# All sixteen magnitude jobs of the last phase run inside its scan loop, their results parked in the normalised-input buffer

## What is computed

```python
xn = _layernorm(x, axis=-1)
# attention-like part
delta = softplus(einsum('btd,ed->bte', xn, Wd) + bd)
a_pos = softplus(a_log) + 0.0001
def step(state, inp):                       # over time
    x_t, delta_t = inp
    dt = delta_t[:, :, None]
    a_bar = jnp.exp(-dt * a_pos[None])
    state = a_bar * state + dt * b_param[None] * x_t[:, :, None]
    return (state, state.sum(-1))
attn = einsum('btd,ed->bte', y, Wo) + bo
# magnitude part
real = einsum('bti,io->bto', xn, cos(theta + theta_noise))
imag = einsum('bti,io->bto', xn, sin(phi + phi_noise))
ffn = sqrt(real * real + imag * imag)
out = x + attn + ffn
```

## Time and profile before

| | us |
|---|---|
| median of 3 runs | 1110.69 |
| lowest and highest run | 1108.01, 1128.71 |
| the profiled execution | 1109.44 |
| its span, slowest core (core 0) | 1107.5 |
| spans of the eight cores | 1095.8 to 1107.5 |

### The profile page before, as it was taken

How to read it: one execution, slowest core, us unless ns; L and a number is a source line. 1 busy time by engine, 2 the same in 40 slices (tenths; PEclk the granted TensorE clock), 3 DMA queues, 4 the chain that set the end, 5 groups by cost and what they waited for, 6 DMA issues and landing times.

```text
span 1107.5 us, 9304 instructions; the slowest of 8 cores (1095.8 to 1107.5 us)
## 1 busy us (share of the span) xinstructions
PE 578.0 (52%) x2248; PEld 242.3 (22%) x2248; DVE 818.6 (74%) x721; ACT 582.2 (53%) x924; POOL 154.2 (14%) x127
## 2 busy tenths in 40 slices
PE   1323334445467554555545447655655554455785
PEld 1211011111123330222212114433222211121343
DVE  4269888989842349999999992434799999999423
ACT  4775767666633235656665553323366555565330
POOL 2477000000012100000000001211000000000232
PEclk9975565656668765666665668988666556665799
DMA  8777100000011310000000002231000000000023
GB/s 231 214 224 206 43 29 29 28 20 1 0 48 59 122 37 0 1 1 0 1 0 1 0 0 66 85 114 57 29 1 0 1 0 0 1 0 1 29 72 114
DMA packets 36323, 51.65 MB, mean 47 GB/s; under 512 B 3120, under 2 KB 19760, under 8 KB 36272
## 3 DMA queue, kind: packets, MB, share of 16 engines
q1 hardware_dynamic: 33584, 42.68, 13.5%
q0 software_dynamic: 2688, 8.39, 2.2%
HBM read 42.67 MB, written 8.39 MB: 46 GB/s over the span
## 4 chain that ended last, share of the span: by engine, by line
DVE 41%; PE 21%; issue 17%; ACT 16%; DMA 2%; DVEq 1%; POOL 0%; ACTq 0%; SPq 0%; POOLq 0%
DVE grot L807 34%; ACT abar L758 9%; PE pd L930 6%; PE pt L649 3%; PE pd L296 3%; PE pt L659 3%; DVE sfm L944 2%; ACT bdg_bf L177 2%; DMA xsub<-xin 1%; PE pe L377 1%; DMA abar<-xin 1%; PE py L958 1%; DVE xsub L439 1%; PE py L377 1%; PE pt L377 1%
## 5 line engine op out<-in xcount | busy, mean ns | idle before, releaser
L807 DVE TENSOR_TENSOR_SCAN grot<-abar,gcar,vbuf 128x768 bf16<-128x768 f32 (+1 forms) x380 | 652.2, 1778 | 43.9 <-ACT abar L758 31.7
L758 ACT ACTIVATE abar<-delta,nega 128x768 f32<-128x768 f32 (+1 forms) x380 | 336.7, 896 | 242.8 <-DVE grot L807 241.2
L845 PE MATMUL pe<-grot,bdg_bf 128*128 128x384 bf16 x256 | 86.8, 444 | 119.2 <-DVE grot L807 119.2
L845 PE MATMUL py<-grot,bdg_bf 128*128 128x384 bf16 x256 | 84.8, 438 | 119.3 <-DVE grot L807 119.2
L296 PE MATMUL pd<-xnbf,wd_bf 128*128 128x384 bf16 (+1 forms) x368 | 97.4, 445 | 20.6 <-ACT xsub L315 14.7
L930 PE MATMUL pd<-ybf,wo_bf 128*128 128x384 bf16 (+1 forms) x320 | 74.8, 385 | 0.0
L832 PE MATMUL py<-grot,bdg_bf 128*128 128x512 bf16 x64 | 33.1, 527 | 79.6 <-DVE grot L807 79.6
L699 POOL TENSOR_TENSOR xsub<-r,i 128x384 f32<-128x384 f32 (+1 forms) x9 | 18.1, 2010 | 384.4 <-ACT i L691 384.4
L649 PE MATMUL pt<-xnbf,cos_bf 128*128 128x384 bf16 (+1 forms) x320 | 70.8, 370 | 0.0
L832 PE MATMUL pe<-grot,bdg_bf 128*128 128x512 bf16 x64 | 34.2, 546 | 68.2 <-DVE grot L807 68.2
L659 PE MATMUL pt<-xnbf,sin_bf 128*128 128x384 bf16 (+1 forms) x320 | 67.8, 359 | 0.0
(11 more groups left out here) (110 smaller groups left out, 566.8 us busy)
## 6 DMA issues: line engine op xcount, KB each, us to landing
xsub<-xin SPq DMA_DIRECT2D x14, 512.0 KB, 4.2
xres<-xin SPq DMA_DIRECT2D x32, 192.0 KB, 2.5
out<-osub POOLq DMA_DIRECT2D x32, 192.0 KB, 2.7
xres<-xin SPq DMA_DIRECT2D x8, 256.0 KB, 3.9
out<-osub POOLq DMA_DIRECT2D x8, 256.0 KB, 3.2
etmp<-tht SPq DMA_DIRECT2D x6, 256.0 KB, 4.8
r<-thn SPq DMA_DIRECT2D x6, 256.0 KB, 5.9
r<-pht SPq DMA_DIRECT2D x6, 256.0 KB, 3.9
```

The lines of the kernel that those rows point to most:

```text
L758: sx = run("scalar", lambda e, sl=sl_ab, par=par, dt=dt, n=n, tp=tp: e.activation(out=abar[:, sl * TP:sl * TP + tp], in_=delta[:, par * TP ...
L807: vs = run("vector", lambda e, g=gsl, sl=sl_ab, par=par, dt=dt, n=n, tp=tp: e.tensor_tensor_scan(out=grot[:, g * TP:g * TP + tp], data0=ab ...
L845: td = run("tensor", lambda e, c=c, g=gsl, dt=dt, n=n, bb=ypair[c]: e.matmul(bb[:, 0:384], bdg_bf[:, (dt * NST + n) * P:(dt * NST + n + 1) ...
```

## The change

For the last phase alone (`p == NPH - 1`):

- `NFC` becomes `nch` (16): the tail issues no job any more.
- The matmuls of job `2*dt` stand at the start of block `dt`. Three entries are added at the end of `aux`: the chain of job `2*dt`, the matmuls of job `2*dt + 1`, the chain of job `2*dt + 1`. In blocks 1 to 6 they come behind Exp 7, 8 and 9; in block 0, which has no copies to `ybf`, behind Exp 5, 6 and 7; in block 7, which has no softplus pieces, behind Exp 3, 4 and 5. The chain at the block's end is gone.
- Jobs 5 to 15 keep their result in 512-column pieces of `xn32` instead of ring slots in `delta`, `vbuf` and `abar` (`P2SLOT`, `rslot2`). POOL waits there for the writers of `xn32` and `xnbf` of the phase and for the product that last read the rows the piece lies in. Jobs 0 to 4 keep their ring slots.

Phases 0 and 1 are as before.

```diff
--- before.py
+++ after.py
@@ -518,8 +518,9 @@
                    + [vbuf[:, j * 512:(j + 1) * 512] for j in range(3)]
                    + [abar[:, j * 512:(j + 1) * 512] for j in range(3)])
         NRING = len(ring_ap)
-        ring_stt = [0] * NRING
-        ring_g = [0] * NRING
+        ring_ap = ring_ap + [xn32[:, 512 * s:512 * s + 512] for s in range(12)]
+        ring_stt = [0] * (NRING + 12)
+        ring_g = [0] * (NRING + 12)
         gadd_ev = [winit_last_g, winit_last_g]
 
         a_done_set = [set() for _ in range(NPH + 1)]
@@ -610,6 +611,13 @@
             ffn_ti = [0]
 
             def ring_avail_waits(j, eng):
+                if j >= NRING:
+                    s = j - NRING
+                    wait(eng, "V", a_x32_v[p])
+                    wait(eng, "S", a_xnbf_s[p])
+                    for r_ in range((512 * s) // TP, (512 * s + 511) // TP + 1):
+                        wait(eng, vv_done[r_][0], vv_done[r_][1])
+                    return
                 if j < 3:
                     par = 0 if j == 0 else 1
                     wait(eng, "T", ev_xT_free[par])
@@ -675,9 +683,17 @@
                     return i
                 return i - NRING + 3
 
+            P2SLOT = {5: 3, 6: 5, 7: 0, 8: 1, 9: 2, 10: 4,
+                      11: 6, 12: 7, 13: 8, 14: 9, 15: 10}
+
+            def rslot2(i):
+                if p == NPH - 1 and i in P2SLOT:
+                    return NRING + P2SLOT[i]
+                return rslot(i)
+
             def emit_ffn_chain(i):
                 dt, c0, wdth = cjobs[i]
-                j = rslot(i)
+                j = rslot2(i)
                 li = i % 2
                 tr, ti = ffn_mm[i]
                 wait("scalar", "T", tr)
@@ -708,10 +724,16 @@
                 mag_exp[i] = run("scalar", lambda e, w=wdth, a=ring_ap[j]: e.activation(
                     out=a[:, 0:w], in_=a[:, 0:w], func=AF.Exp, scale=0.5), "S")
 
-            ffn_at = ({6: [0], 7: [1]} if p == 0
-                      else {0: [0], 1: [1], 2: [2], 3: [3], 4: [4],
-                            5: [], 6: [5], 7: [6]})
-            NFC = 2 if p == 0 else 7
+            if p == 0:
+                ffn_at = {6: [0], 7: [1]}
+                NFC = 2
+            elif p == NPH - 1:
+                ffn_at = {dt_: [2 * dt_] for dt_ in range(NDT)}
+                NFC = nch
+            else:
+                ffn_at = {0: [0], 1: [1], 2: [2], 3: [3], 4: [4],
+                          5: [], 6: [5], 7: [6]}
+                NFC = 7
             yev_pend = []
             for dt in range(NDT):
                 par = dt % 2
@@ -731,6 +753,10 @@
                 if p == 0 and dt < 2:
                     for q_ in range(4):
                         aux.append(("diag", dt + 6, q_))
+                if p == NPH - 1:
+                    aux.append(("fch", 2 * dt, 0))
+                    aux.append(("fmm", 2 * dt + 1, 0))
+                    aux.append(("fch", 2 * dt + 1, 0))
                 if p == 0 and 2 <= dt < 6:
                     aux.append(("sinc", (dt - 2) * 4, 4))
                 if p == 0 and dt in (0, 1, 6, 7):
@@ -797,6 +823,10 @@
                             ev_d = emit_diag_s(adt, ac * 4, ac * 4 + 4)
                             if ac == 3:
                                 bdg_ev[adt] = ("S", ev_d)
+                        elif kind == "fmm":
+                            emit_ffn_mm(adt)
+                        elif kind == "fch":
+                            emit_ffn_chain(adt)
                     if hoisted:
                         vs = hoist_vs[n]
                     else:
@@ -855,8 +885,9 @@
                 for c in ([0] if p == 0 else [0, 1]):
                     yev_mm[(dt, c)] = td_c[c]
                     yev_pend.append((dt, c))
-                for jb in ffn_at.get(dt, []):
-                    emit_ffn_chain(jb)
+                if p != NPH - 1:
+                    for jb in ffn_at.get(dt, []):
+                        emit_ffn_chain(jb)
                 if p == 0:
                     for _ in range(3):
                         if wo_cast_jobs:
@@ -934,7 +965,7 @@
                         start=(k == 0), stop=(k == NDT - 1)),
                         "T" if k == NDT - 1 else None)
                 slot = it % 2
-                jr = rslot(it)
+                jr = rslot2(it)
                 wait("vector", "T", tw)
                 wait("vector", "S", mag_exp[it])
                 wait("vector", "LI", 16)
```

## The result

| | before | after |
|---|---|---|
| median, us (8 runs each) | 1108.74 | 1127.04 |
| lowest and highest run | 1107.19, 1128.71 | 1123.93, 1132.56 |
| the profiled execution | 1109.44 | 1126.31 |
| its slowest core | 0, span 1107.5 | 6, span 1124.8 |
| last phase, scan loop (scan 4 of block 0 to the end of the last scan) | 242.9 | 284.2 |

The ratio of after to before is 1.0164, with a 95% interval of 1.014 to 1.0187: slower, by less than 2%. The run of 1128.71 before and one run of experiment 4 (1116.69) are slow ones and stand in no comparison. The forecast of 1128 was right, and the two halves of the sum have the signs it gave them: +41.3 us in the loop and -24.1 in the tail, together +17.2, against +17.3 in the spans. The rest of the program moved by 0.1 us (scan 4 starts at 789.2 instead of 789.3). After the change the same two lengths stand in seven of the eight cores.

A forecast was written before the change was run, and what follows sets the result against it. VectorE's scans were taken to bound the last phase's loop, TensorE being busy for most of the tail. From 1109.4, +40.3 us in the loop and -21.6 in the tail gave 1128.1 us; range 1120 to 1139.

The forecast's parts named there:

- the two halves of the sum: Last phase: scan loop +40.3 us (35 to 47), tail behind it -21.6 us.
- Rival 2: Tail: TensorE stays at 1.2 GHz, so every step is slow; 1149 us with all slow, chance 0.08.
- Rival 3: Scan loop: bigger stalls, burst never seeing the clock rise and first chain losing cover; 1139 us, chance 0.16.
- Rival 4: Scan loop: ScalarE's three-buffer lead absorbs the second chain, only POOL's 0.70 per added job paid; 1094 us, chance 0.06.
- The stall before scan 10: Last-phase blocks: VectorE waits for Exp 10, queued behind the second chain; 4.95 us a block, used for all eight.
- the burst: Second job's 16 matmuls after scan 7: 4.64 us, the middle of 3.95 and 5.32.
- block 5's 0.70: Block 5 had no chain before, so the first chain's price there is not offset: +0.7 us.
- Blocks 0 and 7: Same 4.95 us stall used though places differ and cover is less; a miss of 1 to 2 us each allowed.
- The first chain behind Exp 7: Blocks 1 to 6: no wait before scan 8; price 0.70 us, offset by 0.70 saved at the block's end.
- The 0.36 us of cover: Before scan 8: product and copy between scans 7 and 8 hide the first chain with 0.36 us to spare.
- The tail: Behind the loop, without jobs: first sum at 1037.0, one 4.28 interval and 14 of 2.76; -21.6 us.
- The rule cited in the prediction: TensorE clock: full clock earned by continuous work, lost through idle gaps; taken strictly, tail gains 0.3 us, not 21.6.

The follow-up runs named there:

- experiment 4: Changed kernel with the matmuls of the last phase's eight odd jobs left out, chains kept (output not the reference's): profiled execution 1095.95 us.
- experiment 1: Changed kernel with the odd job's chain moved from behind Exp 9 to the block's end, its matmuls unmoved: 1093.32 us.
- experiment 7: Experiment 2 with the odd job's POOL add waiting for scan 15, its Ln and Exp behind the next block's Exp 9: 1084.87 us, 0.9779 of before.
- Experiment 2: Changed kernel with odd chains at the block's end and first chains behind Exp 7 in blocks 0 and 7 too: 1093.30 us, 0.9874 of before.
- experiment 5: Kernel before without the last phase's jobs 7 to 15, the tail re-adding magnitudes of jobs 0 to 6 (output not the reference's): 1084.79 us.
- 6: Experiment 2 without POOL's add in the last phase, ScalarE taking Ln of the first square plus 1 (output not the reference's): 1080.59 us.
- experiment 3: Changed kernel with the odd job's chain two Exps later (behind Exp 11 in blocks 1 to 6), its matmuls unmoved: 1102.76 us.

## Why the prediction was right, step by step

The chance stood at 0.72 for a time within 2%, the range held, and rivals 2, 3 and 4 did not happen. But four terms were off: two made the forecast too low, by 3.4 and 1.3 us, two too high, by 3.6 and 2.5. The signs, the place of the stall and the range are earned; that 1128 and 1127 lie so close is luck. Lengths of the blocks (block 0 from scan 4 on), us:

| block | 0 | 1 | 2 | 3 | 4 | 5 | 6 | 7 | sum |
|---|---|---|---|---|---|---|---|---|---|
| before | 24.21 | 31.54 | 31.54 | 32.01 | 31.54 | 30.90 | 31.54 | 29.60 | 242.9 |
| after | 27.06 | 36.84 | 37.29 | 37.42 | 37.48 | 37.57 | 37.50 | 33.02 | 284.2 |
| more | 2.85 | 5.30 | 5.75 | 5.41 | 5.94 | 6.67 | 5.96 | 3.42 | 41.3 |
| forecast | 4.95 | 4.95 | 4.95 | 4.95 | 4.95 | 5.65 | 4.95 | 4.95 | 40.3 |

- **The stall before scan 10: right in mechanism, too small.** Over blocks 1 to 6 it is 33.1 us instead of 6 x 4.95 = 29.7, 11% more. In block 1 the links from the end of scan 7 (831.20) are, in the prediction's order, 0.15 + 0.59 + 5.02 + 0.10 + 2.39 + 0.43 + 1.09 = 9.77 against the 9.41 that it summed; less 4.46 that is 5.31. The mis-sized term is the burst: 4.64 was taken as the middle between 3.95 and 5.32, and it was 5.02 in block 1, 5.27 in block 2 (868.99 to 874.26) and 5.33 in block 5. Timeline of TensorE in block 2, core 6, the cos matmuls at the block's start and the burst after scan 7; then, from experiment 1 (core 6, block 1), a burst at the same place:

```profile
857.35 1.46 PE L657 MATMUL pt<-xnbf,cos_bf 128*128 128x384 bf16 x8
...
868.99 2.76 PE L657 MATMUL pt<-xnbf,cos_bf 128*128 128x384 bf16 x8
871.55 2.71 PE L667 MATMUL pt<-xnbf,sin_bf 128*128 128x384 bf16 x8
```
```profile
825.61 2.48 PE L657 MATMUL pt<-xnbf,cos_bf 128*128 128x384 bf16 x8
827.92 1.46 PE L667 MATMUL pt<-xnbf,sin_bf 128*128 128x384 bf16 x8
```

  At the block's start the job's matmuls stand behind the 16 of the projection and run at 2.4 GHz (granted clock 1.00), 1.46 us for eight. After scan 7 they come behind single pairs, and the granted clock is 0.50 in the first half of the burst and 0.54 in the second: it rises only at its end. That isn't a property of the place. In experiment 1 a burst at the same place took 3.77 (825.61 to 829.38, mean clock 0.73), in experiment 7 such bursts took 3.8 to 5.3, and in the kernel before the projection, which also stands behind single pairs, took 3.95, 4.12, 4.19, 4.36, 4.59 and 5.23 in its six blocks (core 0). Where in a burst the clock rises differs from block to block. What the middle of two rows could not show is that in this kernel, with blocks of 37.3 to 37.6 us, the bursts of blocks 2 to 6 all took 5.27 to 5.33, on every core. Why the clock always rose so late there isn't shown.
- **Late TensorE at block starts: missing from the sum.** In blocks 2 to 6 scan 4 starts 0.2 to 0.4 us late, on `py` or `pe` (the row at 860.61). It needs the `grot` buffer of scan 0, so the pair of scan 0 must be done, and that pair stands behind 32 matmuls in TensorE's queue. They stood there before as well; what is new is how long the projection takes, since the clock rises later in it. Timelines of TensorE: before, core 0, block 3, and after, core 6, block 2 (block 2 before: 3.95):

```profile
876.07 5.23 PE L296 MATMUL pd<-xnbf,wd_bf 128*128 128x384 bf16 x16
```
```profile
852.55 4.96 PE L296 MATMUL pd<-xnbf,wd_bf 128*128 128x384 bf16 x16
```

  In the traces of all nine kernels, on all cores, a block with job matmuls at its start has the wait where the projection takes more than 4.8 us, and hasn't where it takes less; block 5 of experiment 5, with no job there, has none even at 5.32. Before it was block 3 alone, with 0.48; now it is blocks 2 to 6 (4.96 to 5.18). Net 1.3 us. With the longer stalls (33.1 instead of 29.7) and block 5's 0.70, which was right, blocks 1 to 6 cost 35.0 and not 30.4.
- **Blocks 0 and 7: over-priced by 3.6 us.** The prediction used 4.95 and allowed a miss of 1 to 2 each, without the sign. In block 0 the second chain stands behind Exp 7, under the product's cover, and its sin matmuls take 1.46 at the full clock: the wait before scan 8 is 1.41. In block 7 the second job's burst runs at the full clock as well, and its chain costs a wait of 0.61 and 0.69 on a scan; the first chain, behind Exp 3, costs a wait of 2.27 and 0.54 on a copy. Experiment 2 shows what moving the first chain under the product's cover saves: 0.7 in block 0 and 1.7 in block 7.
- **The first chain behind Exp 7: right.** No wait before scan 8 in blocks 1 to 6, POOL's add 2.28 us, price 0.70. The 0.36 us of cover held.
- **The tail: right in kind, 2.5 us better.** The first sum comes 4.88 after the last scan (4.8 by the prediction's sum). No interval was slow (1.5), and a step is 2.69, not 2.76 (15 x 0.07 = 1.0). The 0.07 is in the wait before the sum, 0.60 instead of 0.67. I take it to be one semaphore wait less on VectorE: the program issues a wait only where the event isn't known to be past already, and in after all magnitudes are. Two rows bear it out. In experiment 5 the only step of 2.75 among the 2.69 ones is the one that reads job 6, whose root is the last of the loop; and in experiment 7, as in 1, 2 and 6, it is the last, of job 15, the only one finished behind the loop:

```profile
1074.78 0.62 DVE L992 SCALAR_TENSOR_TENSOR sfm<-pd,csts,xn 128x384 f32<-128x384 f32 x1 [0.60 <-PE pd L978]
...
1077.54 0.62 DVE L992 SCALAR_TENSOR_TENSOR sfm<-pd,csts,xn 128x384 f32<-128x384 f32 x1 [0.67 <-PE pd L978]
```

  That the extra wait itself takes the 0.07 is argued, not tried.
- **Rival 2, the tail at 1.2 GHz.** The mechanism exists, but ends after three steps at most. Core 5 of experiment 2, VectorE's second and third sum, TensorE's transposes at either clock, and then the table of stretches of the same core:

```profile
1041.45 0.62 DVE L978 SCALAR_TENSOR_TENSOR sfm<-pd,csts,xsub 128x384 f32<-128x384 f32 x1 [1.86 <-PE pd L964]
...
1045.75 0.62 DVE L978 SCALAR_TENSOR_TENSOR sfm<-pd,csts,xsub 128x384 f32<-128x384 f32 x1 [1.86 <-PE pd L964]
```
```profile
1042.21 0.88 PE L992 MATMUL py<-csts,sfm 128*128 128x128 f32 x3 [0.87 <-DVE sfm L978]
...
1053.51 0.52 PE L992 MATMUL pe<-csts,sfm 128*128 128x128 f32 x3 [0.87 <-DVE sfm L978]
```
```profile
1042.00:1046.00 4.00, 3.44 (x11) 1.70 (x11) 0.87 (x3) 0.00 (x0) 0.76 (x1) 0.50 0.24 76
...
1050.00:1060.00 10.00, 6.57 (x41) 4.05 (x42) 4.49 (x8) 0.00 (x0) 2.28 (x3) 0.98 0.45 137
```

  At a clock of 0.50 sums are 4.30 us apart, and TensorE stands idle for 0.87 in each step; after three such steps it is at 0.98 and stays there with the same 0.87 idle in each step of 2.69. Three steps cost 3 x 1.61 = 4.8 us. The rule cited in the prediction (the Trainium skill, TensorE: Matmul & The Clock Gate, section Why this matters for your kernels) wants continuous work to reach the full clock; word for word that doesn't hold here, since the clock rose through a gap in every step. What the page says of losing the clock is about long idle gaps only, which the prediction left out; the gaps here are under 1 us, and the clock held through them, as the page has it. How many slow steps a tail has (0, 1, 2 or 3) differs from kernel to kernel and core to core; what decides it is left open.
- **Rival 3** (1139) had the burst right (5.3), but charged 0.7 a block for a lost cover that held, and made blocks 0 and 7 dearer where they were cheaper. **Rival 4** (1094) is near what experiment 1 gives (1093.32), though its mechanism did not happen: the lead of three buffers did not absorb the chain where it stood, and POOL's 0.70 per job is the price only once the order is mended.

## What to carry to other kernels

Work put into a gap of an engine that looks idle (ScalarE was busy 140 of 243 us) costs by where it stands in that engine's queue: everything behind it waits until its latest input is there. Count from the event that releases its producer, not from its own length, and put it where the next consumer has to wait anyway, or split it so that each piece stands behind its input. When a burst on TensorE is priced, read many such bursts and not two: 16 matmuls of 384 columns behind single pairs took 3.8 to 5.3 us here, by where the clock rose in them, and in the changed kernel nearly all lay at the upper end. So give such a term its whole range.

## What the runs showed of the hardware that I had not expected

**POOL's add and VectorE's instructions take turns.** VectorE's scans 8 and 9 and POOL's add in experiment 4, then VectorE's scan 11 and copy and POOL's add in experiment 3 (timelines, core 0 and core 1):

```profile
827.31 1.81 DVE L837 TENSOR_TENSOR_SCAN grot<-abar,gcar,vbuf 128x768 bf16<-128x768 f32 x1
829.04 2.49 DVE L837 TENSOR_TENSOR_SCAN grot<-abar,gcar,vbuf 128x768 bf16<-128x768 f32 x1
828.48 1.43 POOL L715 TENSOR_TENSOR etmp<-r,i 128x384 f32<-128x384 f32 x1 [3.84 <-ACT i L707]
```
```profile
832.65 1.80 DVE L839 TENSOR_TENSOR_SCAN grot<-abar,gcar,vbuf 128x768 bf16<-128x768 f32 x1
834.55 0.71 DVE L850 COPY gcar<-grot 128x4 bf16<-128x4 bf16 x1
833.32 1.92 POOL L715 TENSOR_TENSOR etmp<-r,i 128x384 f32<-128x384 f32 x1 [8.47 <-ACT i L707]
```

An add that starts during a scan ends 0.8 to 0.9 us after that scan's end, however long the scan still had to run (829.91 against 829.12, 835.24 against 834.45). In the last-phase loops of all nine kernels, on all cores, 696 adds started during a scan that had another scan behind it, 0.1 to 1.5 us before its end: each ended 0.78 to 0.87 after it, and the next scan took 2.48 to 2.57 us. The scan under way keeps its 1.8 us; the instruction behind it pays, a scan with 2.49 instead of 1.80, a copy of four columns with 0.71 instead of 0.17. So the add's own length, up to 2.3 us beside scans and 0.99 alone, is the rest of the running scan plus its work, and VectorE loses 0.5 to 0.8 us once for each add. Where VectorE stands idle for the length of the add, as in experiment 7, it loses nothing. The Trainium skill (SBUF — State Buffer, section SBUF: two separate sides) has this as a rule: GpSimd and a VectorE instruction with two SBUF inputs hold a common pair of ports by an exclusive lock, and the one that comes second waits for the whole instruction of the first. The scans, with two inputs, agree: the add waits for the end of the scan under way. The copy has one input and pays as well; the page gives the lock also to VectorE instructions in a 2-port mode, which a copy can enter, and no run here shows in which mode this one ran.

**TensorE at 2.4 GHz kept that clock through gaps**: in the tail after the change it did 27.29 us of work in 40.30, idle for 0.87 in each step of 2.69, at a granted clock of 0.99.
